# The last stage of a two-layer attention and feed-forward kernel on one core: head weights held in TensorE, values moved past them, one pipeline stage less

## The reference, cut to what matters

```python
# attention: q = layernorm(x), k = v = ctx; d_mat = exp(log_d - m), m the row maximum
scores = jnp.einsum('bhtd,bhsd->bhts', q, k) * (1.0 / np.sqrt(DH))
s_mat = scores * d_mat
denom = jnp.maximum(jnp.abs(jnp.sum(s_mat, axis=-1, keepdims=True)), jnp.exp(-m)) + BACKEND_EPS
h = jnp.einsum('bhts,bhsd->bhtd', s_mat, v) / denom
rrms = jax.lax.rsqrt(jnp.mean(h * h, axis=-1, keepdims=True) + NORM_EPS)
x = x + h * rrms * gain                     # heads side by side: 256 columns
# feed-forward: xt = layernorm(x)
gate = jax.nn.softmax(xt @ gate_w.T, axis=-1)
base = xt @ weight.T
t = jnp.einsum('nh,erh->ner', xt, lora_U)
x = x + base + jnp.einsum('ne,eor,ner->no', gate, lora_V, t) / R
```

## Time and profile before

| | |
|---|---|
| median of 3 runs | 385.65 us (385.58 to 385.9) |
| the profiled execution: its time, its span | 385.09 us, 383.3 us |
| mean granted TensorE clock, share of full speed | 0.990 |
| busy: PE, DVE, ACT, POOL | 326.1, 297.4, 283.5, 235.2 us |
| PE weight loads busy (beside PE) | 225.1 us |
| last stage, first head values to the end of the span | 283.2 to 383.3 us |

### The profile page before, as it was taken

The page is one execution under the profiler, slowest core; times in us unless marked ns, Lnnn a source line. Parts: engine busy times, 40 slices in busy tenths (PEclk is TensorE's granted clock), DMA queues, the critical chain, the costliest instruction groups (busy, mean ns, idle before and its releaser), DMA issues.

```text
span 383.3 us, 9007 instructions
## 1 busy us (share of the span) xinstructions
PE 326.1 (85%) x2933; PEld 225.1 (59%) x2933; DVE 297.4 (78%) x1014; ACT 283.5 (74%) x594; POOL 235.2 (61%) x278
## 2 busy tenths in 40 slices
PE   7899789999999999756767778678877999999976
PEld 6777566766767665424445545446445666666654
DVE  3899755786988986898998998986446787787884
ACT  5666486677667787837798989887668888888753
POOL 1213543877888897578998898982005546546560
PEclk9999999999999999989899999999999999999999
DMA  7999999999956600000000000000001212212101
GB/s 228 287 286 270 258 226 206 251 215 255 206 109 150 120 1 5 1 0 0 0 2 3 1 0 2 1 2 0 2 15 29 43 43 44 56 43 43 43 16 55
DMA packets 44141, 33.67 MB, mean 88 GB/s; under 512 B 19904, under 2 KB 40256, under 8 KB 43968
## 3 DMA queue, kind: packets, MB, share of 16 engines
q1 hardware_dynamic: 44096, 33.11, 36.1%
HBM read 24.71 MB, written 8.39 MB: 86 GB/s over the span
## 4 chain that ended last, share of the span: by engine, by line
PE 41%; DVE 26%; issue 17%; ACT 8%; DMA 4%; POOL 2%; SPq 1%; DVEq 0%; POOLq 0%; ACTq 0%
PE PS L1751 4%; DVE sm L812 4%; PE PS L1743 4%; PE PS L1409 4%; DMA QT<-scr_k 3%; PE PS L1515 3%; DVE sm L784 3%; PE PS L1481 3%; PE PS L1490 3%; PE PS L1572 3%; PE PS L1713 2%; PE PS L1498 2%; PE PS L1736 2%; DVE negm L673 2%; PE PS L1702 2%
## 5 line engine op out<-in xcount | busy, mean ns | idle before, releaser
L673 DVE TENSOR_REDUCE negm<-PS 128x4 bf16<-128x512 f32 x64 | 41.0, 685 | 13.1 <-PE PS L1490 12.9
L1166 ACT ACTIVATE pT<-PS 128x512 f32<-128x512 f32 x64 | 36.4, 595 | 16.7 <-PE PS L1481 15.9
L499 POOL TENSOR_TENSOR kst<-kst,rows 128x1024 f32<-128x1024 f32 x16 | 38.0, 2372 | 7.9 <-ACT kst L1229 7.9
L1306 ACT ACTIVATE lnT<-PS,Atok 128x128 f32<-128x128 f32 x128 | 36.5, 370 | 2.0 <-DVE lnb L930 0.8
L1621 PE MATMUL PS<-identf,w2f 128*128 128x128 f32 x128 | 17.9, 284 | 18.2 <-ACT w2f L1252 18.2
L516 POOL TENSOR_TENSOR kst<-kst,rows 128x1024 f32<-128x1024 f32 x14 | 33.1, 2367 | 0.0
L538 POOL TENSOR_TENSOR smd<-smd,mhalf 128x1 f32<-128x1 f32 x16 | 9.0, 564 | 37.0 <-DVE smd L998 37.0
L1515 PE MATMUL PS<-pT,vx 128*32 128x128 f32 x512 | 27.3, 285 | 1.8 <-ACT pT L1166 1.8
L544 POOL TENSOR_TENSOR rr<-ms,mhalf 128x8 f32<-128x8 f32 x16 | 26.3, 1646 | 1.9 <-DVE ms L1012 1.9
L1621 PEld LDWEIGHTS PS<-identf,w2f 128*128 128x128 f32 x128 | 14.1, 143 | 22.6 <-ACT w2f L1252 22.4
L930 DVE SCALAR_TENSOR_TENSOR lnb<-PS,lnT 128x512 f32<-128x512 f32 x32 | 20.6, 683 | 8.1 <-PE PS L1713 5.9
(11 more groups left out here) (237 smaller groups left out, 1014.8 us busy)
## 6 DMA issues: line engine op xcount, KB each, us to landing
scr_q<-qpart SPq DMA_DIRECT2D x8, 384.0 KB, 3.5
scr_k<-kpart SPq DMA_DIRECT2D x8, 384.0 KB, 4.6
X<-in_x SPq DMA_DIRECT2D x8, 256.0 KB, 4.9
CTXT<-in_ctxT SPq DMA_DIRECT2D x8, 256.0 KB, 4.7
vx<-in_ctx SPq DMA_DIRECT2D x16, 128.0 KB, 2.7
out<-rest SPq DMA_DIRECT2D x16, 128.0 KB, 1.7
rows<-in_rows SPq DMA_DIRECT2D x1, 1544.0 KB, 14.2
qst<-scr_q SPq DMA_DIRECT2D x8, 192.0 KB, 5.3
```

The source lines that it names most:

```text
L499: gp.tensor_tensor(n2[q.slot], n2[q.slot], ln2g, ALU.mult).then_inc(b_g2, 1)
L673: v.tensor_reduce(negm[f.slot % 2][:, 4 * hg:4 * hg + 4], PS[:, 2 + hg % 2, :].rearrange("p (h k) -> p h k", h=4), AX_X, ALU.max, negate=T ...
L1166: s.activation(pT[:, hg, :], PS[:, hg % 2, :], ACT.Exp, scale=float(DH0) ** -0.5).then_inc(a_e, 1)
L1306: last = s.activation(dT[half][:, cols], PS[:, half, cols], ACT.Exp, scale=1.0, bias=Atok[:, n.b, h:h + 1])
```

## The change

`values` now takes the weights `smT` (128 columns a head) as the stationary operand and moves the first 33 columns of `vx2`. The result lies with rows on the partitions, as `yc` wants it, so `value_columns`, `yTc` and `back` go, and `head_values` reads bank 6. The pipeline has five stages: n = t, a = t-1, c = t-2, e = t-3, d = t-4. `scores` and `weights` are done for n rather than for a; on PE `scores` stands just ahead of `wide_all`. DVE's `norms` is split into `row_stats`, `denominators` and `mean_squares`, which are no longer laced, and `weights` stands last in the turn. The turned gates go to bank 5 beside the scores instead of bank 6. The drain is written anew, with six `keep_busy` products in place of two.

```diff
             def values(a):
                 pe.wait_ge(c_ld[a.slot % 2], 16 * (a.b // 2 + 1))
                 pe.wait_ge(c_sm, a.b * 2 + 2)
+                done(pe, c_y, a, 0)
                 for h in range(H1):
-                    last = t.matmul(PS[64 * (h % 2):64 * (h % 2) + 64, 6, (h // 2) * 128:(h // 2 + 1) * 128],
-                                    vx2[a.slot % 2][:, h, :], smT[h // 4][:, (h % 4) * 128:(h % 4 + 1) * 128],
-                                    start=True, stop=True)
+                    last = t.matmul(PS[:, 6, 64 * h:64 * h + DH1 + 1], smT[h // 4][:, (h % 4) * 128:(h % 4 + 1) * 128],
+                                    vx2[a.slot % 2][:, h, 0:DH1 + 1], start=True, stop=True)
                 last.then_inc(c_pv, 1)
...
-            def back(b):
-
-                pe.wait_ge(c_yT, b.b + 1)
-                pe.wait_ge(c_d, min(b.b * 2 + 3, 2 * NB))
-                done(pe, c_y, b, 0)
-                for i in range(4):
-                    last = t.transpose(PS[:, 0, i * 128:(i + 1) * 128], yTc[:, i * 128:(i + 1) * 128], identf[:])
-                last.then_inc(c_t4, 1)
...
-            def value_columns(a):
-                act.wait_ge(c_pv, a.b + 1)
-                done(act, c_t4, a, 0)
-                s.activation(yTc[:], PS[:, 6, :], ACT.Copy).then_inc(c_yT, 1)
...
             def head_values(b):
-                act.wait_ge(c_t4, b.b + 1)
+                act.wait_ge(c_pv, b.b + 1)
```

The turn of DVE:

```diff
+            def turn_cd(n, a, c, _e, d):
                 if d:
                     gate_max(d)
                     gated(d)
+                if c:
+                    heads(c)
+                    new_rows(c)
+                    row_stats(c)
                 if a:
+                    denominators(a)
+                if d:
+                    finish(d)
+                if a:
+                    mean_squares(a)
+                if n:
+                    weights(n, 0)
+                    weights(n, 1)
```

The turn of POOL:

```diff
+            def turn_cd(_n, a, c, _e, _d):
                 if c:
                     row_power(c)
+                if a:
+                    gained(a)
+                    head_power(a)
```

More of the change, by code:

```diff
@@ L1016, in turn_cd, with row_stats @@
-            def turn_cd(_n, a, b, c, _e, d):
+            def row_stats(c):
+                k1.start(c)
+                zc = smd[c.slot % 2]
+                dve.wait_ge(c_x, c.b + 1)
+                take_wait()
+                c_bn = k1.mark(v.bn_stats(zc[:, 8:14], X[:, c.b, :]))
+                dve.wait_ge(d_c1, c_bn)
+                done(dve, d_r, c, -1)
+                take_wait()
+                c_var = k1.mark(v.bn_aggr(zc[:, 0:2], zc[:, 8:14]))
+                dve.wait_ge(d_c1, c_var)
+                v.tensor_scalar(zc[:, 4:5], zc[:, 0:1], -1.0, None, ALU.mult)
+                v.tensor_scalar(zc[:, 2:3], zc[:, 1:2], EPS, None, ALU.add).then_inc(d_w, 1)
+                k1.end()
@@ new lines, in denominators @@
+            def denominators(b):
+                cc.start(b)
+                yb_l = yc[b.slot % 2][:, :, DH1]
+                dve.wait_ge(c_y, b.b + 1)
+                done(dve, c_ms, b, 0)
+                b_neg = cc.mark(v.scalar_tensor_tensor(out=den[:, :, 0], in0=yb_l, scalar=-1.0, in1=EM[:, b.b, :],
+                                                       op0=ALU.mult, op1=ALU.max))
+                dve.wait_ge(c_ch, b_neg)
+                b_abs = cc.mark(v.tensor_tensor(den[:, :, 1], den[:, :, 0], yb_l, ALU.max))
+                dve.wait_ge(c_ch, b_abs)
+                b_den = cc.mark(v.tensor_scalar(den[:, :, 2], den[:, :, 1], 5e-5, None, ALU.add))
+                dve.wait_ge(c_ch, b_den)
+                cc.mark(v.scalar_tensor_tensor(out=den[:, :, 3], in0=den[:, :, 2], scalar=1e-6, in1=den[:, :, 2],
+                                               op0=ALU.mult, op1=ALU.mult))
@@ new lines, in mean_squares @@
+            def mean_squares(b):
+                dve.wait_ge(c_sq, b.b + 1)
+                b_sum = cc.mark(v.tensor_reduce(den[:, :, 0], hsq[b.slot % 2][:].rearrange("p (h e) -> p h e", h=H1),
+                                                AX_X, ALU.add))
+                done(dve, c_rr, b, -1)
+                dve.wait_ge(c_ch, b_sum)
+                v.scalar_tensor_tensor(out=ms[b.slot % 2][:], in0=den[:, :, 0], scalar=1.0 / DH1, in1=den[:, :, 3],
+                                       op0=ALU.mult, op1=ALU.add).then_inc(c_ms, 1)
+                cc.end()
@@ L1683, in log_d @@
                 done(pe, c_d, n, -1, 2, half + 1)
-                if half == 0:
-                    done(pe, c_y, n, -1)
-                else:
-                    done(pe, d_xT, n, -3)
+                if half == 1:
+                    done(pe, d_xT, n, -2)
                 hs = n.slot * H1 + 4 * half
```

214 lines of the change are left out of this document (60 added, 154 removed).

## The result

| | before | after |
|---|---|---|
| median of 4 runs, us | 385.68 (385.58 to 385.9) | 394.62 (393.86 to 395.29) |
| the profiled execution: its time, its span | 385.09, 383.3 | 395.29, 393.6 |
| mean granted TensorE clock | 0.990 | 0.970 |
| busy: PE, PE's loads, DVE, ACT, POOL | 326.1, 225.1, 297.4, 283.5, 235.2 | 334.1, 238.8, 304.9, 272.6, 235.7 |

The changed kernel is slower by 2.3% (ratio 1.023, 95% interval 1.021 to 1.025). A full turn of the last stage, which answers to the earlier trace rows, is now 5.97 us long; the windows show one, and three stretches of the ends. The columns are as in rows 1: stretch, length, then busy time with the number of instructions for PE, PE's loads, DVE, ACT and POOL, then the granted clock, the DMAs' share and GB/s.

A forecast was written before the change was run, and what follows sets the result against it. The prediction took PE's stream to bound the kernel before, and the loop through `finish` after. A last wide product 8.2 us later, less 1.6 in the drain, gave 391.7 for the profiled execution, median 392.2, range 386.5 to 398.5.

The forecast's parts named there:

- the likeliest case: Full turns take the long loop's 6.17 us, with a range of its own of 390 to 394; chance 41%.
- The removed work: Per turn PE loses the 0.53 us turning back, about 0.1 of which stays; ACT loses a 0.6 us copy nobody awaits.
- The head values: On PE, 16 full-width weight loads at 0.11 us apart take 1.76 us, where the block took 1.02.
- Rival 2: Head values' loads hide beneath short products, block 0.5 us instead of 1.76: faster, 382.2 us; chance 12%.
- The loop: Wide product through head values' loads, gates' transpose, gtT, yc, denominators and finish to the next wide product: 6.17 us a turn.
- DVE's own loop: DVE's operations of one turn in the new order sum to 5.75 us, where before it was 5.17.
- PE alone: PE's own stream sums to 6.05 us, less some 0.3 for tile-shape changes: 5.75, level with now.
- Rival 3: The long loop is shorter than reckoned, so DVE's 5.75 us sets the turn: 387.2 us; chance 16%.
- Rival 1: POOL's product `gained` holds up DVE's last denominator by 0.5 us: 6.67 us a turn, 398.2 in all; chance 22%.
- the costing of the fill: At the pipeline's start, three turns of 5.14 us lead from first head values at 283.18 to the fourth at 298.6.
- The drain: From the loop's last wide product to DVE's end takes 17.1 us instead of 18.73, saving 1.6, given 0 to 3.

The follow-up runs named there:

- e3: The changed kernel with 64 moving columns a head instead of 33, the extra results unused; median 394.4 us.
- e11: The kernel before with the new head-value form, idle products in the fill, and both logarithm halves ahead of experts and head values on PE; median 388.55 us.
- e2: The changed kernel with ACT's copy of the head values (yc) ahead of the gates' copy (gtT), the squares behind both; median 394.75 us.
- e6: The changed kernel with POOL's product `gained` moved ahead of `row_power`; median 401.48 us.
- e1: The changed kernel with 20 idle products of 512 columns on PE where it stood still in the fill; median 392.43 us.
- e5: The changed kernel with the drain's six idle products behind item 13's experts replaced by nine ahead of item 14's rows; median 395.25 us.
- e8: The changed kernel with 20 idle products in the fill, three for six ahead of item 14's rows, and ACT's `normed_rows(b14)` ahead of `gate_exp(b13)`; median 391.37 us.
- e10: The changed kernel with the old form of the head values, its copy and turning back put into the five stages; median 408.4 us.

## Why the prediction was right, and where its sizes were off

The forecast was 392.2 us in 386.5 to 398.5, slower with 83%; it is 394.62, 0.6 above the 390 to 394 of the likeliest case. The profiled execution was to take 391.7 and took 395.29, 3.6 more. By the marks that the prediction set:

| stretch | predicted | after | difference |
|---|---|---|---|
| first head values start at | 283.18 | 281.96 | -1.2 |
| to the fourth head values | 15.4 | 20.67 | +5.3 |
| to the last wide product of the loop | 72.0 | 70.18 | -1.8 |
| to DVE's end | 17.1 | 18.53 | +1.4 |

- **The removed work.** PE's turning back and ACT's copy are gone; ACT's busy time fell by 10.9 us and nobody gained by it, as forecast.
- **The head values.** 16 loads at 0.11, 1.76 us, were 1.86, 0.116 each. That this pair of loads would scale from two to 16 held. Rival 2 (hidden loads, faster) is refuted by these 1.86 us, and e3 shows that the moved columns do not set them. The Trainium skill (TensorE: Matmul & The Clock Gate, LDWEIGHTS (loading the stationary operand)) has a load's time go with its columns, P / 1.2 ns, 107 ns for 128; the trace has 116 with the steps between at the full clock. At the lower clock it has 221 (3.54 us for 16), which that figure does not give; there the measurement decides. The Trainium skill's figure of some 60 cycles for a short product (TensorEngine Tiling (Array Packing), Instruction Overhead), on which the prediction's rival 2 draws, did not bind.
- **The loop.** This was the mechanism, and it held. Each mark but the last came within 0.11 us of the forecast: loads at w + 2.02 (2.05), the gates' transpose done at 4.15 (4.14), gtT at 4.18 (4.19), yc at 4.35 (4.46), finish at 5.50 (5.60); the next wide product came at 5.96 (6.17). PE's loads stood idle ahead of it for 0.29, where some 0.5 was forecast. Two terms were too large: ACT starts yc 0.17 after gtT though gtT takes 0.28 (I had added whole durations), and the first load costs nothing beyond the signal. That is 12 turns of 0.2, 2.4 us too many. DVE's own loop of 5.75 was reached by no run, so that sum is not shown.
- **PE alone.** The prediction's "so 5.75: level with now" was wrong: e11 shows 5.94. The 0.3 that was to vanish with changes of tile shape was 0.1, or 0.2 if the loads are put in at their measured 1.86. It did not matter to the sum, as the loop through `finish` is longer. Rival 3's 387.2 had DVE's 5.75 as the next bound, and with the copies in rival 3's order (e2) a turn is still 5.935.
- **Rival 1** was missed by 0.1 us in full turns: the last denominator starts at 342.41 and `gained` at 342.51. By the prediction's own marks `gained` would have come first, at w + 5.45 against 5.52; it came at 5.50 against 5.40. So that the likeliest case came out in full turns is in part luck. e6 shows the collision and its size (0.37 a turn). The Trainium skill (SBUF — State Buffer, Who interferes with whom) has a DVE instruction with two SBUF inputs and a GpSimd one that reads SBUF exclude one another; with `gained` the trace agrees, 0.55 against 0.18.
- **The step that failed** is the costing of the fill: three turns of 5.14 at full clock, with nothing that holds up the denominators. Measured, the three took 20.67 us, not 15.4. The larger part is the clock. "The clock was 1.00 in full turns; gaps of 0.5 us should not change that" is true of full turns, but the fill was costed at full clock as well. There PE stood idle for 1.86 us ahead of item 1's head values, and from 289.4 to 303.1 the clock was at its lower level. e1 takes 16.6 us from the first to the fourth head values where the change took 20.67, and 6.00 where it took 6.57 for the turn behind, so this cost 4.6.
- **The rest of the fill.** At full clock, in e1, the three turns are still 1.2 longer than forecast. Most of that is rival 1's collision, which the prediction looked for in full turns alone: in e1 one denominator of item 0 takes 0.55 and one of item 2 0.68, 0.9 us more than the two take unheld. The chain from the denominators through the weights to the next head values passes through them.
- **The drain** was to save 1.6 and saved 0.2. The gates' product of item 15 was put done at 14.0; in the change the maximum that waits for it starts at 388.33, 15.5 after the wide product, and in e5 at 387.32, 13.6. So the chain was about right, and what came on top is the slow clock (0.50 from 381.6 to 385.0), after item 14's rows had waited 2.2 us for ACT, with the idle products behind it.

Together: -1.2 for the earlier start, +1.2 and +4.6 in the fill, -2.4 for the turn, +1.4 in the drain, 3.6. Errors of both signs cancel here, and that the total came so near is in part luck. The sign is not: e1, whose profiled execution holds the clock in the fill, is still 6.9 us slower in the median than the kernel before. Against that kernel the profiled execution is 10.2 us longer up to DVE's end: -1.2 for the start, 2.8 for the fill's three turns at full clock (16.60 in e1, 13.79 in the kernel before), 4.6 for the clock, 4.2 for the turns behind, -0.2 for the drain.

What stays open: why e1, with 4.6 us won in its fill, is only 2.2 below the change in the median. The spread of the fill between executions, 2.5 to 4.6 us, and the falls elsewhere in e1 and e8 would go far to explain it, but only the profiled execution of each kernel can be read stretch by stretch.

## What to carry to other kernels

Where the short side moves and the long side is stationary, count the weight loads: with 128 columns they take 0.116 us each, with 33 or 64 columns moving, and two heads that share the array half by half are cheaper than one that fills it. When work is reordered, follow the loop through the consumer that frees the bank: an operation that was early and free (`finish` here) becomes the bound when it stands behind a wait for a copy. And look at the ends of a pipeline as closely as at its full turns, with the clock beside them: in the profiled execution the slow clock in the fill cost 4.6 us, as much as 0.4 us in each of the twelve turns.

## What the runs showed of the hardware that I had not expected

- In the fill (284 to 288) PE was busy for 2.14 us of 4.00, and its granted clock then went from 1.00 to 0.50 for 13.7 us, though PE was busy for 13.1 of these at the lower level. The kernel before, with 3.06 of 4.00 and then 2.95 of 4.00 from 280 to 288, stayed at 1.00. But e3's clock fell at 284.9, after 3.04 of 4.00 (280 to 284), so PE's busy share over these stretches does not tell the kernels apart. In full turns idle gaps of 0.29, and in e10 of 0.93 on PE, left the clock at 1.00.
- The weight loads slow down with the clock: 16 of them take 1.86 us at 1.00 and 3.54 at 0.50.
- Two ACT instructions in a row start closer than the first one takes: yc 0.17 after gtT, which shows as 0.28.
- POOL's short power on one column (`smd<-smd,mhalf`, 341.74 for 0.56) reads two SBUF operands and did not hold up the DVE maximum at 341.99, which took 0.18; the 256-column product did. So the rule of the Trainium skill (SBUF — State Buffer, Who interferes with whom), read as all or nothing for any such pair, is not what this trace shows; which part of a POOL instruction's shown span reads SBUF stays open, and the spans shown for POOL are rough.
